# Moving the expert routing and the row scatter into the time-mix stage, with one list of expert tiles between two and six groups of shared experts

## What is computed

```python
x = x + attention(layernorm(x)) + ffn(layernorm(x))      # layer 0
xn = layernorm(x)
x = x + time_mix(xn) + experts(xn)                       # layer 1

# time_mix: k, v, r from blends of each token with the one before, then a scan over tokens
xk = x * mix_k + x_prev * (1 - mix_k)      # the same for v and r
k, v, r = xk @ W_k.T, xv @ W_v.T, sigmoid(xr @ W_r.T)
new_p = max(p, u + k_t); wkv_t = (exp(p - new_p) * q + exp(u + k_t - new_p) * v_t) / (sum of both)
p, q = max(p + w, k_t), exp(p + w - p2) * q + exp(k_t - p2) * v_t
y = r * wkv;  time_mix = y @ W_o.T

# experts: 8 routed experts of width 128, two per token, and a shared one of width 256
probs = softmax(xn @ router); the two largest of a token are its coefficients
experts = sum over its two experts of coef * (silu(xn @ gate_e) * (xn @ up_e)) @ down_e  + shared expert
```

## Time and profile before

| what | value |
|---|---|
| median of 3 runs | 1778.17 us (1774.63 to 1780.77) |
| the profiled execution, its own time | 1778.28 us |
| its span, first to last instruction | 1776.5 us |
| VectorE busy | 1332.9 us (75%) |
| TensorE busy | 1351.6 us (76%) |
| ScalarE busy | 983.0 us (55%) |
| GpSimd busy | 508.0 us (29%) |

### The profile page before, as it was taken

One profiled execution on the slowest core, in us unless ns is written; L12 is line 12 of the kernel. 1 busy time (PEld: TensorE's weight loads), 2 busy tenths in 40 slices (PEclk: granted clock), 3 DMA queues, 4 the chain that ended last, 5 costly groups with the idle time before them and its releaser, 6 DMA issues. The chain is left out here.

```text
span 1776.5 us, 28410 instructions
## 1 busy us (share of the span) xinstructions
PE 1351.6 (76%) x9622; PEld 605.3 (34%) x9622; DVE 1332.9 (75%) x1954; ACT 983.0 (55%) x1299; POOL 508.0 (29%) x598
## 2 busy tenths in 40 slices
PE   5874897888889888888988878987475663789960
PEld 2443322222222222222222225665133332358750
DVE  7996777978779878897989615787799973775662
ACT  3554255777768767786878874563144431226640
POOL 3764000110102010010201103221375642563275
PEclk9887568999889999998999988999688776899995
DMA  6576301040312303131220226665301015777773
GB/s 197 166 236 195 83 8 38 13 92 5 70 39 36 73 5 78 27 70 38 44 65 8 41 71 168 190 198 183 112 12 47 24 36 158 244 259 245 228 249 118
DMA packets 155575, 185.21 MB, mean 104 GB/s; under 512 B 19380, under 2 KB 130484, under 8 KB 154420
## 3 DMA queue, kind: packets, MB, share of 16 engines
q1 hardware_dynamic: 147864, 162.40, 32.7%
q0 software_dynamic: 7296, 20.98, 3.5%
q10 hardware_dynamic: 288, 0.20, 0.1%
HBM read 99.89 MB, written 83.36 MB: 103 GB/s over the span
## 5 line engine op out<-in xcount | busy, mean ns | idle before, releaser
L1174 ACT ACTIVATE att_prob<-att_score,late_score_scale 128x1024 f32<-128x1024 f32 (+3 forms) x640 | 594.4, 988 | 228.9 <-PE att_score L1276 226.7
L1145 DVE TENSOR_REDUCE att_m_part<-att_mx 128x2 f32<-128x1024 f32 (+3 forms) x408 | 473.3, 1160 | 103.5 <-PE att_mx L1217 53.2
L1260 PE MATMUL att_pv<-att_prob,att_v 128*32 128x512 f32 (+3 forms) x2560 | 325.1, 582 | 0.5 <-POOL att_prob L1109 0.2
L1109 POOL TENSOR_SCALAR_AFFINE_SELECT att_prob<-att_prob 128x256 f32<-128x256 f32 x256 | 102.9, 407 | 777.0 <-ACT att_prob L1174 776.7
L1276 PE MATMUL att_score<-att_qop,att_kop 50*128 50x512 f16 (+3 forms) x1280 | 262.1, 370 | 8.9 <-ACT att_prob L1174 6.0
L1211 PE MATMUL att_mx<-att_kop,att_qop 48*128 48x512 f16 (+3 forms) x944 | 182.5, 369 | 103.6 <-DVE att_m_part L1145 99.9
L1145 DVE TENSOR_REDUCE att_m_part<-att_mx_one 128x1 f32<-128x384 f32 (+1 forms) x336 | 220.8, 657 | 40.9 <-PE att_mx_one L1211 33.7
L1276 PEld LDWEIGHTS att_score<-att_qop,att_kop 50*128 50x128 f16 x1280 | 70.0, 95 | 290.1 <-ACT att_prob L1174 187.5
L1211 PE MATMUL att_mx_one<-att_kop,att_qop 48*128 48x384 f16 (+1 forms) x336 | 135.0, 402 | 19.6 <-DVE att_m_part L1145 16.2
L1211 PEld LDWEIGHTS att_mx<-att_kop,att_qop 48*128 48x128 f16 x944 | 52.1, 97 | 174.0 <-DVE att_m_part L1145 157.7
L1868 PE MATMUL rwkv_prod<-rwkv_xm,late_mixT 128*128 128x512 f32 x192 | 91.4, 630 | 20.3 <-DVE rwkv_xm L1768 19.7
(11 more groups left out here) (262 smaller groups left out, 2170.7 us busy)
## 6 DMA issues: line engine op xcount, KB each, us to landing
moe_xt<-rows SPq DMA_DIRECT2D x46, 256.0 KB, 3.8
results<-moe_y SPq DMA_DIRECT2D x46, 256.0 KB, 3.0
qk<-qkv_parts SPq DMA_DIRECT2D x32, 256.0 KB, 3.2
va<-qkv_v SPq DMA_DIRECT2D x8, 1024.0 KB, 5.4
att_v<-va SPq DMA_DIRECT2D x8, 1024.0 KB, 5.1
moe_xp<-parts SPq DMA_DIRECT2D x28, 256.0 KB, 4.0
rows<-att_zeros SPq DMA_DIRECT2D x8, 864.0 KB, 6.2
att_kop<-qk SPq DMA_DIRECT2D x48, 128.0 KB, 4.9
```

Of the source, the lines that this page charges most:

```text
L1109: nc.gpsimd.affine_select(out=at, in_=at, compare_op=ALU.is_ge, fill=0.0, base=0, pattern=[[0, 2], [1, P]], channel_multiplier=-1)\
L1145: nc.vector.tensor_reduce(cells[:, sides[0]:sides[-1] + 1, some], bank.rearrange("p a (h w) -> p a h w", w=w), AX.X, ALU.max).then_inc(m_f ...
L1174: nc.scalar.activation(prob[:, r % (PROBS * HP), :, n0:], score[:, r % 2, :, n0:], ACT.Exp, scale=late_weights.score_scale[:, 0:1])\
L1260: op = nc.tensor.matmul(pv[at, n0:], v[:, slot, j, at], prob[:, (st * HP + h // 2) % (PROBS * HP), h % 2, n0:], start=(j == 0), stop=(j == ...
```

## The change

- **Routing and scatter move into the time-mix stage.** TensorE makes the logits after the products of groups 0 (two groups) and 1 (six groups), VectorE does the routing in three pieces at the ends of its steps 2, 3 and 4, and GpSimd, which then has nothing else to do, scatters from there on. The rows come in eight chunks through two buffers; SyncE loads them between the loads of `x` and the stores of the output. The two buffers of the logits' inputs are loaded in a row in SyncE's step 2, each load waiting for the logits two groups earlier, and the load of `x` for group 3 stands behind them.
- **Products on VectorE, scalings on ScalarE.** The six scalings a group go from GpSimd to ScalarE (`past`). The outcome is written as `y = ((q - v) * sigmoid(d) + v) * r`: one sigmoid less on ScalarE, five products and sums of 1,024 columns a group on VectorE instead of two, none on GpSimd. k, v, r share four accumulators in turn instead of six; loops are written out; the output goes out by halves.
- **One part.** `PARTED = (32,)`: 39 tiles instead of 46, and no gather before the last tile is stored.
- **Order of the expert stage.** Two groups of the shared expert, all weight splits and `owners` (which expert each tile has), the 39 tiles, then six groups of the shared expert while GpSimd gathers; VectorE adds two or three pairs of token tiles after each group, and the output products of the last two groups come after the last pair. SyncE issues the stores of `out`.

The core of the diff (`below_top`, `choice` and `places` are the old `routing` and `places` in three pieces; `past` and `gates` are ScalarE's, the last two pieces TensorE's):

```diff
-PARTED = (20, 12)
+PARTED = (32,)
...
+        return s.signals
...
+            def load_x(n):
+                b, use = n % B, n // B
+                after(sp, xm_done, NW * (n - B + 1))
+                sp.dma_start(x[:, b], xnT_d[:, :, b, use * GT:use * GT + GT + 1]).then_inc(x_in[b], 16)
+
+            def load_parts(g):
...
+            def load_rows(c):
+                after(sp, xs_out[c % XP], 16 * TOP * TG * (c // XP))
...
+            load_x(0)
+            load_x(1)
...
+            def step(m, at):
+                if m >= B and at[0] is not None:
+                    load_x(at[0])
+                if m == B:
+                    for g in range(XP, G):
+                        load_parts(g)
+                    for c in range(XP):
+                        load_rows(c)
...
+            pool.wait_ge(placed, 2)
+            for c in range(CHUNKS):
+                pool.wait_ge(xs_in[c % XP], 16 * (c // XP + 1))
+                for i in range(TG):
+                    j = c * TG + i
+                    part = max(part for part in range(PARTS) if PART_AT[part] <= j)
...
+                nc.vector.tensor_tensor(e_new[:, b], e_new[:, b], v, ALU.mult).then_inc(times_v, 1)
...
+                nc.vector.tensor_tensor(y[:, b], q[:, b, :, 0:GT], v, ALU.subtract).then_inc(wkv_done, 1)
+                dve.wait_ge(wkv_done, 3 * n + 1)
+                nc.vector.tensor_tensor(y[:, b], y[:, b], d[:, b], ALU.mult).then_inc(wkv_done, 1)
+                dve.wait_ge(wkv_done, 3 * n + 2)
+                nc.vector.tensor_tensor(y[:, b], y[:, b], v, ALU.add).then_inc(wkv_done, 1)
+                dve.wait_ge(wkv_done, 3 * n + 3)
+                nc.vector.tensor_tensor(y[:, b], y[:, b], r, ALU.mult).then_inc(y_done, 1)
+
+            def step(m, at):
+                for stage, n in zip((blend, state, outcome), at):
+                    if n is not None:
+                        stage(n)
+                if m == ROUTED - 2:
+                    below_top()
+                if m == ROUTED - 1:
+                    choice()
+                if m == ROUTED:
+                    places()
...
+            def past(n):
+                b = n % B
+                act.wait_ge(x_in[b], 16 * (n // B + 1))
+                after(act, prod_done, NO * (n - B + 1))
+                for w in range(NW):
+                    for c in range(KC):
+                        op = nc.scalar.activation(xm[:, b, w, c], x[:, b, c, 0:GT], ACT.Identity, scale=unmix[:, w, c:c + 1])
+                    op.then_inc(prev_done, 1)
+
+            def gates(n):
+                b = n % B
+                act.wait_ge(arg_done, n + 1)
+                nc.scalar.activation(d[:, b], d[:, b], ACT.Sigmoid)
+                nc.scalar.activation(e_old[:, b], e_old[:, b], ACT.Exp)
+                nc.scalar.activation(e_new[:, b], e_new[:, b], ACT.Exp, scale=-1.0).then_inc(gates_done, 1)
...
+                if m + 1 < G:
+                    past(m + 1)
+                if old is not None:
+                    gates(old)
+                if m == ROUTED - 1:
+                    act.wait_ge(route, 2)
+                    nc.scalar.activation(ex[:, :, :], z[:, :, :], ACT.Exp, scale=scales.unscale[:, 0:1]).then_inc(exp_done, 1)
...
+                if m == 0:
+                    pe.wait_ge(expert_weights.split, expert_weights.ROUTER_SPLIT)
+                    for g in range(XP):
+                        route_logits(g)
+                if m == 1:
+                    for g in range(XP, G):
+                        route_logits(g)
+                if m == ROUTED - 1:
+                    count_chosen()
...
+            shared(0)
+            down_weights(slice(SHARED, SHARED + E))
+            for e in range(E):
+                weights(e)
+            shared(1)
+            shared_out(0)
+            owners()
+            shared_out(1)
...
+            LATER = G - FIRST
+            left = PAIRS - pairs[0]
+            for i, n in enumerate(range(FIRST, G)):
+                if i >= 2:
+                    shared_out(n - 2)
+                shared(n)
+                finish(left * (i + 1) // LATER - left * i // LATER)
+            for n in range(G - 2, G):
+                shared_out(n)
...
+            for n in range(FIRST):
+                shared(n)
+            for n in range(FIRST):
                 shared_out(n)
+            turn(0)
...
+            shared(FIRST)
+            for n in range(FIRST, G):
+                if n + 1 < G:
+                    shared(n + 1)
+                shared_out(n)
```

More of the change, by code:

```diff
@@ L2000, in moe_phase, with after, groups @@
-        UNITS = G * SHARED
-        block = ctx.enter_context(nc.Block())
-        def part_of(n):
-            return max(part for part in range(PARTS) if TILE_AT[part] <= n)
-        def after(eng, step, n):
-            if n >= 0:
-                eng.wait_ge(step.sem, step.done(n))
+        block = ctx.enter_context(nc.Block())
+        def after(eng, sem, count):
+            if count > 0:
+                eng.wait_ge(sem, count)
+        def groups(step, depth):
+            for m in range(G + depth - 1):
+                step(m, [m - k if 0 <= m - k < G else None for k in range(depth)])
@@ L2071, in _ @@
+            groups(step, 5)
+            for h in range(2):
+                sp.wait_ge(out_stored[h], 16 * G * HALVES // 2)
         @block.gpsimd
         def _(pool):
[L2073 to L2080 removed]
+            nc.gpsimd.memset(expert_weights.ones[:, :], 1.0).then_inc(expert_weights.ones_set, 1)
@@ L2291, in _ @@
             dve.wait_ge(down_high, 1)
             down_weights(slice(0, SHARED))
-            routing()
-            places()
-            for n, g in enumerate(ORDER):
-                if n >= 2:
-                    shared_out(n - 2, ORDER[n - 2])
-                shared(n, g)
-                weights(n)
-                if n == 2:
-                    owners()
-                if n == 4:
-                    down_weights(slice(SHARED, SHARED + E))
-            for n in range(G - 2, G):
-                shared_out(n, ORDER[n])
+            shared(0)
@@ L2312, in _ @@
                 tile_low(n)
-                if pair < PARTED[0] // 2 and n == TILE_AT[1] + 5 + pair * 7 // 4:
-                    finish(pair)
-                    pair += 1
-            for rest in range(pair, NT // 2):
-                finish(rest)
+                if pairs[0] < PARTED[0] // 2 and n == TILE_AT[1] + 5 + pairs[0] * 7 // 4:
+                    finish(1)
+            LATER = G - FIRST
[7 more added lines that the diff above has]
+                shared_out(n)
         @block.scalar
@@ L2329, in high, with shared @@
                 nc.scalar.copy(dst, hid[:, n % 2, cols]).then_inc(high_done.sem, 1)
+            def shared(n):
+                if n >= 2:
+                    after(act, down_done, down(n - 2))
+                for u in range(SHARED):
+                    activate(unit(n, u), slice(0, GT), scales.unscale[:, w.GATE:w.GATE + 1])
+                    if u > 0:
+                        high(unit(n, u - 1), hid_p[:, n % 2, 0, u - 1], slice(0, GT))
+                high(unit(n, SHARED - 1), hid_p[:, n % 2, 0, SHARED - 1], slice(0, GT))
             def tile_x(n):
@@ L2452, in _ @@
             pe.wait_ge(down_low, 2)
-            after(pe, base_done, G - 1)
-            turn(0)
             before = None
```

884 lines of the change are left out of this document (432 added, 452 removed).

## The result

The changed kernel takes **1712.1 us**, the median of 4 runs (1706.4 to 1717.6); beside it the kernel before takes 1776.4 (4 runs, 1774.4 to 1780.8). The ratio is 0.9635, 95% interval 0.9592 to 0.9677. The profiled execution has a time of 1717.6 and a span of 1715.1, so it is itself 5.5 us above the median.

The account below looks back on a forecast made before the run. VectorE was taken to bound the time-mix stage, TensorE the tiles, and GpSimd's gathers with VectorE's additions the tail. Terms of -2 (time-mix), -75 (expert start), -26 (tiles) and +58 (tail) gave -45 from 1778.2: 1733 us, range 1715 to 1757.

Parts of the forecast that it names:

- the last term of the tail: Program end: 9.6 us from the last sum to the end, 10.5 before, with a shorter way from SyncE.
- the term for the stages ahead of the time-mix stage: All stages before the time-mix stage: length unchanged at 1262.6 us, a gain of 0.
- the start of the expert stage: Expert stage up to the first tile: 113.8 us becomes 39, a gain of 75, as logits, routing and scatter leave.
- the scatter's wait for VectorE: Time-mix stage: each scatter waits out VectorE's current operation, mean 0.48 us, so 1.74 us a scatter while VectorE runs.
- VectorE's step: Time-mix stage: one VectorE step takes 20.5 us in place of 25.0, priced with GpSimd idle.
- the scatter was to end the stage: Time-mix stage: the scatter, not the output, ends it at 1482, 2 us earlier than before.
- tiles at 102.9 against 103.1: Expert tiles: 39 tiles at 2.58 us each take 103.1 us instead of 129.2, a gain of 26.
- Rival 4: Time-mix stage: blends stay at 10.3 us and the step does not shrink, 1774 us in all; chance 0.03.
- rival 3: Tail: TensorE at half clock bounds it, six shared groups taking 94 us, not 80; 1747 us; chance 0.10.
- rivals 2 and 5: Time-mix stage: scatters wait about 1 us each, 1748 us, chance 0.14; or starve until VectorE ends, 1796 us, chance 0.04.
- rival 1: Time-mix stage: the scatter is not slowed, the output ends the stage, gathers save 3 us; 1721 us; chance 0.18.
- The tail: After the last tile: gathers no longer hidden under tiles, 108 us against 49.6, a loss of 58.

Follow-up runs that it names:

- e3: The kernel before with its eight result stores issued by SyncE instead of GpSimd: 1838.0 us, against 1851.4 for the kernel before on that chip.
- e4: The changed kernel with the last of its eight result stores issued by GpSimd instead of SyncE: 1739.4 us, kernel before there 1851.4.
- f2: The kernel before with only the six scalings of a step moved from GpSimd to ScalarE: 1760.1 us, against 1770.0 for the kernel before there.
- f5: The kernel before with only the three products of a step moved from GpSimd to VectorE: 1747.6 us, against 1770.0 for the kernel before there.
- f3: The kernel before with scalings moved to ScalarE and products to VectorE, routing and scatter not moved: 1733.2 us, against 1770.0 there.
- e1: The changed kernel with two parts of 20 and 12 blocks instead of one, second kind of chip: 1742.2 us, kernel before there 1851.4.
- h0: The changed kernel with two parts of 20 and 12 blocks instead of one, first kind of chip: 1699.9 us, changed kernel there 1714.7.
- g2_both: The changed kernel with two parts, x of group 3 loaded ahead and four row buffers, second kind of chip: 1743.9 us, changed kernel there 1741.0.
- r1_after: The changed kernel, nothing altered, run as a mark on the second kind of chip: 1741.0 us, kernel before there 1852.0.
- h2_after: The changed kernel, nothing altered, run as a mark on the first kind of chip: 1714.7 us, kernel before there 1775.0.

## Why the prediction was wrong, and what of it was right

**The steps that failed.** The forecast time was 1733 and the measured one is 1712.1. The step that failed most plainly is the last term of the tail, "9.6 to the end (10.5 today, with a shorter way from SyncE)": it is 3.4 us. The runs e3 and e4 show why: the end costs 3.3 to 4.4 us behind the last operation where SyncE issues the last store and 9.5 to 10.5 where GpSimd does. The second is the term for the stages ahead of the time-mix stage, put at nothing without a range: they are 5.3 us shorter. It took both to leave the range: with 6.2 or with 5.3 us more the time would be 1718.3 or 1717.4, inside it. The third is the start of the expert stage, 34.3 us against 39. And one mechanism was wrong without a trace in the sum, the scatter's wait for VectorE.

By stretches, 5.3 us of the 21 lie in the stages ahead, 2.0 in the time-mix stage, 4.7 in the start of the expert stage, 0.2 in the tiles and 4.4 in the tail. The rest, some 4.5, is the profiled execution, which lies 5.5 us above its own median.

**Right in kind.** VectorE's step was said to be 20.5 and is 20.05; VectorE was to be through 198.9 us after the stage's start and is after 197.7; the scatter was to end the stage and does; tiles at 102.9 against 103.1, with the rate that the earlier trace rows gave; the gathers run without a hole of GpSimd's, and the six groups fit beneath them. Rival 4 is refuted by f2, f5 and f3, rival 3 by the tail (58.7 us of TensorE in 103), rivals 2 and 5 by the scatters.

**The scatter's port waits, mis-sized.** I gave each scatter a mean wait of 0.48 us, 24 us in all. The 64 took 97.4 us from first to last, of which 12.8 are waits for rows; the rest, less 64 times 0.96 and 0.30 between them, leaves some 4.5. The step that failed is "each scatter first waits for the rest of the current one": it takes the starts as random, while in the rows above, where both engines have a period of 1.26 us, one scatter after another starts just ahead of VectorE's next operation and does not wait. By the scatter alone rival 1 came true. Its gain did not, for two things that the sum lacked took it back: the waits for rows (12.8, with two buffers) and GpSimd's end of a stage (7.2 us behind its last instruction, not the 2.7 of the landing). -24 + 4.5 + 12.8 + 4.5 is -2.2; the stretch is 2.0 shorter than forecast. That the stage came out within 2 us is luck: its errors cancel.

**The start of the expert stage, 4.7 us too long.** VectorE had finished group 0 after 14.0 us (15 in the sum). The sixteen splits took 6.4 us (7.7 in the sum: 0.48 each, but neighbours overlap and stand 0.40 apart, as I had allowed for the blends and not here). The largest part is behind `owners`, which ended after 32.3 us: from there to the first tile's products it is 2.0 us, not 4.

**The tail, 4.4 us too long.** The end is the term, 9.6 us against 3.4. Against it stand 2.6 us more in the gathers (84.6 against 82) and 1.1 less to the first one.

**5.3 us from the stages ahead, forecast as none.** The fewer arrays that are filled with zeros are not the cause: e1 and h0, with two arrays again, have the same attention stage (823.4 and 823.3 us). From its first to its last product (first and last start) that stage takes 829.3 us in the kernel before, 829.0, 826.2 and 822.4 in f2, f5 and f3, whose edits all come later, and 824.0, 823.5, 823.6, 815.5 and 816.8 in five profiles of the changed kernel or e4; g2_both, a version of the changed kernel, has 829.7, as the kernel before. The granted clock goes with it (0.93 at 829, 0.94 at 824, 0.95 at 815.5). So it moves by some 14 us between profiles, and whether the 5.3 us belong to the change at all is open. What sets it was not found.

## What to carry to other kernels

Price an engine's operation by a row where its neighbour is idle, and a moved transfer by what it leaves behind as well: who issues the last one before a stage or the program ends decides here over some 5 to 6 us. Don't average port waits over random starts when both engines have a fixed period; look whether they lock. And where a change adds cover (six groups over the gathers), ask again whether what was merged still pays: here the split list gains 15 us more on the first kind of chip, and nothing on the second.

## What the runs showed of the hardware

**A GpSimd that issued last ends late.** Where GpSimd comes last, the stage ends 7.2 us after its last scatter instruction, and the program 9.5 to 10.5 us after the operation ahead of its last store. Where SyncE issues the last store, it is 2.6 us after ScalarE's last copy and 3.3 to 4.4 after the last operation. What GpSimd's end waits for was not tested.

**On the chips of the second kind engines stand still beside GpSimd's indirect transfers.** This is TensorE in the changed kernel on one of them (r1_after), while GpSimd issues gather after gather:

```profile
1663.88 0.59 PE L102 MATMUL moe_gate_ps<-moe_xp,experts_shared_p 128*128 128x512 f16 x1 [1.52 <-issue]
1666.68 0.59 PE L102 MATMUL moe_gate_ps<-moe_xp,experts_shared_p 128*128 128x512 f16 x1 [2.21 <-issue]
1669.48 0.59 PE L102 MATMUL moe_gate_ps<-moe_xp,experts_shared_p 128*128 128x512 f16 x1 [2.21 <-issue]
1672.28 0.59 PE L102 MATMUL moe_gate_ps<-moe_xp,experts_shared_p 128*128 128x512 f16 x1 [2.21 <-issue]
```

A product of six matmuls that takes 1.46 us in the same place on the first kind (h2_after) issues one matmul each 2.8 us, waiting for nothing that the profile shows. By the table the stretches with such transfers beside other work grow (tail 102 to 120 us, tiles with gathers 131 to 162 in the changed kernel and to 179.5 in e3, the start with scatters 112 to 136 in e3), and those without don't (tiles 104.6 on both kinds, start 32 to 34). The kernel before has more of such overlap and loses some 75 us there, the changed one some 27: hence a ratio of 0.964 to 0.969 on the first kind and 0.941 or 0.942 on the second. The mechanism was not tested.
